# A graph layer beside a transformer on one core: the edge sort moved out of the input pass

## The chip, the cores and the metric

The kernel runs on one core of a Trainium2 chip. The metric is the time on the device in microseconds (us), as the median of several runs; lower is better. A profile of one execution belongs to it.

## The reference

For 6250 nodes of 256 features the kernel computes three things and adds them to the input. The first is an attention over 100,000 edges that go in by source node:

```python
feats = einsum('nd,hdo->hno', x, Ws) + bs            # 4 heads of 64
score = a_s[:, src] + a_d[:, dst] + aw_e * elem + ab
w = exp(-relu(score / 20))
pooled = segment_sum(w * feats[:, dst], src)         # by source node
out = pooled / segment_sum(w, src)
```

The second is a transformer of four layers on the same nodes, each with a linear attention (softmax of the queries over 32 features, of the keys over all nodes, one context matrix per head) and a feed-forward part of 1024 with GELU. The third is a slice attention on the sum of both. All is float32.

## The kernel before

All inputs are normalised first. Nodes are worked on in 50 tiles of 125 rows, in 13 groups: twelve of four tiles and one of two. There are six passes: the input pass (features of the graph layer, keys, queries and context of layer 0, and the table of features in DRAM), four layer passes (`attend`, `up`, `down`, and in the first three the keys, queries and context of the next layer), and the slice attention with its output. Layers are counted from 0; the first layer pass is layer 0, the last is layer 3.

The edge work is done beside the transformer, and that is what this case is about. It has three parts.

- The **sort** (`sort_step`, line 854) sorts edges by blocks of source tiles, on VectorE, in 59 steps. Steps 0 to 3 load and prepare; steps 4 to 28 count one pair of tiles each, with four passes over 125x800 (lines 884 to 888); step 32 (`COUNT_STEP`) makes prefix sums with two matmuls (line 1451) and a table of tiles that SP brings back from DRAM (line 515); steps 33 to 58 give each edge its place, 13 steps for each half of the edges, eight operations on 125x400 each (lines 926 and 927).
- The **scatter** (line 658): 800 indirect DMAs of GpSimd, 400 after each half is placed, write the records of the edges to DRAM in sorted order. Then `edges` loads them (line 525) and `rows` transposes the row numbers and stores them (line 529).
- The **edge blocks**: 220 blocks of 512 edges, in 224 pipelined items `("edge", k)`. Item k on TensorE makes the products of block k-4 (line 1486, eight matmul records) and the scores of block k-2 (line 1475); on VectorE it adds the sums (line 1154), makes the scores (958 to 963), the one-hot matrices (945, 951), and weighs the gathered features (941), which TensorE's item k+1 needs. GpSimd gathers features four blocks ahead (line 627). SP loads the rows of block k+2 in item k (line 445); line 951 waits for that.

All engines go through one list, `order`. It is made by hand: `stages` holds the transformer's stages with a cost in us that the author gave each (line 66 on), and `beside` holds the edge work with due times in the same clock. A beside item goes into the list before the first stage that begins at or after its due time. Each engine works the list in order. `mixed` is the planner's time at which the input pass ends (248.1), `added` that at which the last layer ends (2432.7). Before, sort steps are due from 20.0 on, every 16.0 in the input pass and every 7.5 behind it. The records are loaded 1.45 us for each of the 800 scatters behind the first half's last step; blocks are due evenly from there to `added`.

SP issues all other loads and stores in the order of the list too. Before each group of a layer it fetches the residual rows (line 412) and the stored queries (line 435) of the next group.

Of the kernel before, what the change touches and what calls it, by code (L numbers as in the profile page):

```python
# [10 lines left out]
def build_program(nc, x, src, dst, edge_weight, Ws, bs, aw, ab, Wq, Wk, Wv, Wo, bo, ln1_g, ln1_b, W1, b1, W2, b2,  # L11
# [46 lines left out]
    COUNT_STEP = 4 + NT // 2 + 3  # L58
# [31 lines left out]
    mixed = now()  # L90
# [26 lines left out]


    beside = []
    at = 20.0  # L120
    for k in range(SORT_STEPS):
        beside.append((at, ("sort", k)))
        at += 16.0 if at < mixed else 7.5
        if k == COUNT_STEP + HALF_STEPS:
            sorted_half = at
    edges_at = sorted_half + 1.45 * EC + 10.0
# [3 lines left out]
        beside.append((edges_at + 45.0 + k * (added - edges_at - 45.0) / (NB + 4), ("edge", k)))  # L130
    order, at = [], 0.0
    for item, us in stages:
        while beside and beside[0][0] <= at:
            order.append(beside.pop(0)[1])
        order.append(item)
        at += us
# [1485 lines left out]
```

How the kernel before makes its waits and increments, by code:

```python
            def load_x(p, s, source):  # L402
                slot, _ = x_loaded(p, s)
                if use(p, s) >= 3:
                    before = divmod(use(p, s) - 3, NGR)
                    if before[0] <= DEPTH:
                        e.wait_ge(*x_stored(*before))
                    else:
                        e.wait_ge(join_set, before[1] + 1)
                    if before[0] < DEPTH:
                        e.wait_ge(h1_set, nth(*before))
                e.dma_start(tiles_of(x_of(p, s), s), node_rows(source, s)).then_inc(slot, 16)
# [14 lines left out]
            def fetch(l, s):  # L427
                e.wait_ge(*x_stored(l, s))
                load_x(l + 1, s, x_d[l % 2])
                e.wait_ge(d_q, q_stored(l, s))
                if s:
                    e.wait_ge(v_done, v_end("attend", l, s - 1))
                elif l:
                    e.wait_ge(v_done, v_end("attend", l - 1, NGR - 1))
                e.dma_start(by_chunk(qT_in[:, :])[:, :, 0:cols_of(s)], q_rows(s)).then_inc(d_qin, 16)
# [4 lines left out]
            def load_rows_of(j):  # L440
                d_sem, _ = rows_in(j)
                if j >= 3:
                    e.wait_ge(ohT_set, j - 2)
                at = rows_d[TE * j:TE * (j + 1), :].rearrange("t p -> (t p)")
                e.dma_start(rows_ring[j % 3], at.partition_broadcast(R)).then_inc(d_sem, 16)
# [1 line left out]
            def fetch_sw(s):  # L447
# [1 line left out]
                if s < NSW:  # L449
                    e.wait_ge(d_sw, 16 * NGR)
                    e.wait_ge(v_done, v_end("slice_sums", NGR - 1))
                else:
```

## Time and profile before

| | us |
|---|---|
| median of 3 runs | 4057.73 |
| lowest and highest | 4050.81, 4059.79 |
| the profiled execution as a whole | 4050.51 |
| its span, first to last instruction | 4048.8 |
| TensorE busy | 3393.4 (84%) |
| VectorE busy | 2461.3 (61%) |
| GpSimd busy | 1950.4 (48%) |
| ScalarE busy | 1127.3 (28%) |

PE is TensorE, DVE VectorE, ACT ScalarE, POOL GpSimd, SP the engine that issues most DMAs. A line number such as L1486 is that of the kernel above. The busy time of pipelined matmuls overlaps a little. The granted clock (PEclk) is 1.00 for 2.4 GHz; single operations run at that or at 1.2 GHz.

### The profile page before, as it was taken

How to read it: one execution, taken by the hardware profiler on the slowest of the kernel's cores; microseconds unless marked ns; L12 is line 12 of the kernel's file. 1: busy time of each engine (PE TensorE's matmuls, PEld its weight loads, DVE VectorE, ACT ScalarE, POOL GpSimd, SP SyncE). 2: the span in 40 equal slices, each digit the busy share in tenths (PEclk: the TensorE clock that was granted, in tenths of full speed). 3: DMA queues.
4: the chain of work that ended last, by engine and by line, in shares of the span. 5: the costliest groups of instructions: out<-in, count | busy, mean ns of one | idle time of the engine just before them, and what ended most of it. 6: DMA issues, size and time to landing. Idle time of an engine off the chain costs nothing.

```text
span 4048.8 us, 44198 instructions
## 1 busy us (share of the span) xinstructions
PE 3393.4 (84%) x13941; PEld 2388.1 (59%) x13941; DVE 2461.3 (61%) x6828; ACT 1127.3 (28%) x1851; POOL 1950.4 (48%) x1745
## 2 busy tenths in 40 slices
PE   6887899999799999799888888777777677758989
PEld 4564666666566666566566566655455455545557
DVE  6886989644344444344677777665555455548951
ACT  2332232333233333223322222223223222312220
POOL 2120005777677777776356566555455455520000
PEclk8998999999899999899999999888888888979989
DMA  2222111221322222222344444444334434651224
GB/s 94 91 85 87 36 41 42 46 45 31 75 43 43 43 43 40 66 43 46 100 122 120 116 121 116 127 124 126 105 105 111 115 99 112 104 86 55 74 100 150
DMA packets 222382, 337.18 MB, mean 83 GB/s; under 512 B 49106, under 2 KB 175953, under 8 KB 221900
## 3 DMA queue, kind: packets, MB, share of 16 engines
q1 hardware_dynamic: 154316, 215.02, 17.0%
q0 software_dynamic: 67840, 119.33, 15.2%
q8 instruction: 119, 1.95, 0.2%
q14 instruction: 107, 0.88, 0.1%
HBM read 246.73 MB, written 86.62 MB: 82 GB/s over the span
## 4 chain that ended last, share of the span: by engine, by line
PE 57%; DVE 25%; DMA 5%; SPq 5%; issue 4%; ACT 3%; DVEq 1%; ACTq 0%
PE bank_v L1447 16%; PE bank_a L1432 12%; PE bank_e L1486 9%; DMA arena<-edge_rows 3%; PE bank_a L1353 3%; PE bank_v L1376 3%; PE bank_v L1339 3%; PE bank_v L1504 2%; PE bank_v L1594 2%; SPq L412 2%; DVE arena L941 2%; SPq L435 2%; PE bank_a L1280 2%; DVE st L813 1%; PE bank_v L1419 1%
## 5 line engine op out<-in xcount | busy, mean ns | idle before, releaser
L627 POOL DMA_INDIRECT arena<-gather_table,arena x880 | 919.6, 1045 | 769.9 <-PE bank_e L1486 541.5
L658 POOL DMA_INDIRECT edge_records<-acc x800 | 964.7, 1206 | 646.8 <-issue 646.8
L1486 PE MATMUL bank_e<-arena 128*125 128x260 f32 x1760 | 515.0, 442 | 284.1 <-DVE arena L941 284.0
L1432 PE MATMUL bank_a<-hT,W_sb 128*128 128x500 f32 (+1 forms) x1664 | 715.0, 581 | 38.3 <-ACT hT L677 24.7
L1447 PE MATMUL bank_v<-W_sb,gT 128*125 128x256 f32 x3200 | 735.8, 387 | 0.0
L1447 PEld LDWEIGHTS bank_v<-W_sb,gT 128*125 128x125 f32 x3200 | 602.6, 191 | 112.8 <-issue 23.4
L1486 PEld LDWEIGHTS bank_e<-arena 128*125 128x125 f32 x1760 | 355.6, 213 | 352.2 <-DVE arena L941 291.2
L1432 PEld LDWEIGHTS bank_a<-hT,W_sb 128*128 128x128 f32 x1664 | 319.2, 195 | 370.9 <-issue 314.0
L677 ACT ACTIVATE gT<-bank_a,cols 128x500 f32<-128x500 f32 (+1 forms) x416 | 274.4, 661 | 525.4 <-PE bank_a L1432 518.4
L677 ACT ACTIVATE hT<-bank_a,cols 128x500 f32<-128x500 f32 (+1 forms) x208 | 145.5, 748 | 750.7 <-PE bank_a L1280 750.4
L941 DVE TENSOR_TENSOR arena<-arena 128x1024 f32<-128x1024 f32 x220 | 267.7, 1217 | 0.0
L1154 DVE TENSOR_TENSOR acc<-acc,bank_e 125x260 f32 x440 | 184.6, 420 | 132.6 <-PE bank_e L1486 126.9
L1048 DVE TENSOR_REDUCE kst<-bank_a 128x1 f32<-128x500 f32 (+1 forms) x104 | 66.8, 656 | 293.6 <-PE bank_a L1353 293.1
L1115 DVE TENSOR_TENSOR xs<-bank_v,xs 125x512 f32<-125x512 f32 x100 | 69.0, 691 | 283.0 <-PE bank_v L1447 282.4
L762 ACT ACTIVATE arena<-esc 128x16 f32<-128x16 f32 x220 | 47.3, 215 | 656.1 <-DVE esc L963 655.1
L1419 PE MATMUL bank_v<-M_sb,qT_in 128*125 128x256 f32 x800 | 192.6, 395 | 30.7 <-issue 22.1
L1353 PE MATMUL bank_a<-hT,Wqkv 128*128 128x500 f32 (+1 forms) x416 | 184.6, 587 | 34.6 <-ACT hT L677 28.0
L1419 PEld LDWEIGHTS bank_v<-M_sb,qT_in 128*125 128x125 f32 x800 | 157.0, 197 | 63.5 <-issue 28.9
L1376 PE MATMUL bank_v<-h,ek 125*128 125x256 f32 x800 | 189.3, 391 | 0.0
L1142 DVE TENSOR_REDUCE esc<-bank_e 128x16 f32<-128x48 f32 x220 | 45.1, 205 | 232.3 <-PE bank_e L1486 231.1
L1280 PE MATMUL bank_a<-ident,h 125*128 125x125 f32 x900 | 124.4, 283 | 70.5 <-DVE h L837 58.8
L1339 PE MATMUL bank_v<-Wqkv,hT 128*125 128x256 f32 x800 | 181.2, 379 | 0.0
(261 smaller groups left out, 4388.3 us busy)
## 6 DMA issues: line engine op xcount, KB each, us to landing
residual<-xs SPq DMA_DIRECT2D x60, 500.0 KB
xs<-residual SPq DMA_DIRECT2D x60, 500.0 KB
arena<-edge_rows SPq DMA_DIRECT2D x220, 125.0 KB
queries<-qT_out SPq DMA_DIRECT2D x48, 500.0 KB, 3.6
qT_in<-queries SPq DMA_DIRECT2D x48, 500.0 KB, 14.0
arena<-gather_table,arena POOLq DMA_INDIRECT x880, 3.5
edge_records<-acc POOLq DMA_INDIRECT x800
slice_weights<-arena SPq DMA_DIRECT2D x12, 1000.0 KB, 5.0
```

The costliest lines, as they stand in the source:

```text
L627: e.indirect_dma_start(g_of(j)[:, i, :], None, table_d, bass.IndirectOffsetOnAxis(ap=rec[:, TE * j + i, 0:1].bitcast(I32), axis=0))\
L658: e.indirect_dma_start(rec_d, bass.IndirectOffsetOnAxis(ap=pos_i[:, f:f + 1], axis=0), r3[:, f, :], None).then_inc(d_rec, 16)
L677: e.activation(to, of, func, **k).then_inc(a_done, 1)
L941: e.tensor_tensor(gf, gf, bc(g[:, :, HG * DG:ROW].unsqueeze(3), [P, TE, HG, DG]), ALU.mult)\
L1280: o = e.transpose(b[:, i * R:(i + 1) * R], X[:, i, c * P:(c + 1) * P], ident[0:R, 0:R])
L1339: o = e.matmul(b[0:R, i % 2 * D:(i % 2 + 1) * D], hv[:, k, i * R:(i + 1) * R], W[:, k, 0:D], start=k == 0, stop=k == KC - 1)
L1353: o = e.matmul(b[:, 0:n], W[:, k, D + c * P:D + (c + 1) * P], hv[:, k, 0:n], start=k == 0, stop=k == KC - 1)
L1376: o = e.matmul(b[:, c * D:(c + 1) * D], ek[:, a:a + P], h1[:, i * D:(i + 1) * D], start=i == 0, stop=i == tiles(s) - 1)
L1419: o = e.matmul(to, qv[:, k, i * R:(i + 1) * R], M_sb[:, k * D:(k + 1) * D], start=k == 0, stop=k == KC - 1)
L1432: o = e.matmul(b[:, 0:n], W[:, k, f * P:(f + 1) * P], hv[:, k, 0:n], start=k == 0, stop=k == KC - 1)
L1447: o = e.matmul(b[0:R, i % 2 * D:(i % 2 + 1) * D], gv[:, f, i * R:(i + 1) * R], W2_sb[:, f * D:(f + 1) * D], start=False, stop=f == FB - 1 ...
L1486: o = e.matmul(ps_sum[h], oh_ring[j % 4][:, i * R:(i + 1) * R], g_of(j)[:, i, :], start=i == TH * h, stop=i == TH * (h + 1) - 1)
```

## The change

The sort's first step becomes due 20 us before the input pass ends, and all steps follow at 7.5. Three of them still fall into the pass (0, 1 and 2); the others lie in layer 0, into its tenth group. Since the record load and the blocks are placed by the sort's end, they move back by 80.6 planner us, and the 224 items lie at 2.877 instead of 3.237. The second edit keeps step 32, which fills a PSUM bank of its own, from standing between the two halves of a `down` pair, which share one.

```diff
     beside = []
-    at = 20.0
+    at = mixed - 20.0
     for k in range(SORT_STEPS):
         beside.append((at, ("sort", k)))
-        at += 16.0 if at < mixed else 7.5
+        at += 7.5
         if k == COUNT_STEP + HALF_STEPS:
             sorted_half = at
...
     for item, us in stages:
-        while beside and beside[0][0] <= at:
+
+        whole = item[0] != "down" or item[3] % 2 == 0
+        while beside and beside[0][0] <= at and (whole or beside[0][1] != ("sort", COUNT_STEP)):
             order.append(beside.pop(0)[1])
```

## Rows read from the trace of the kernel before

**Rows 1.** The page: busy time by engine, chain that ended last

```profile
PE 3393.4 (84%) x13941; PEld 2388.1 (59%) x13941; DVE 2461.3 (61%) x6828; ACT 1127.3 (28%) x1851; POOL 1950.4 (48%) x1745
...
PE 57%; DVE 25%; DMA 5%; SPq 5%; issue 4%; ACT 3%; DVEq 1%; ACTq 0%
```

**Rows 2.** Stretches of the input pass: length, busy by engine, clock, DMA share, GB/s

```profile
91.50:332.30 240.80, 207.57 (x918) 147.46 (x917) 208.86 (x570) 83.78 (x180) 41.38 (x35) 0.94 0.28 94
170.10:191.40 21.30, 19.68 (x94) 14.24 (x93) 19.23 (x55) 8.14 (x17) 4.83 (x4) 1.00 0.27 92
```

**Rows 3.** Timeline: start, length, operation, in brackets the idle time before

```profile
107.98 1.09 PE L1280 MATMUL bank_a<-ident,h 125*128 125x125 f32 x4 [5.21 <-ACT qT_out L677]
...
102.84 0.58 DVE L862 CAST acc<-acc 125x800 f32<-125x800 int32 x1 [5.57 <-DMA acc<-in_edge_weight]
```

**Rows 4.** Stretches of layer 0: seven groups, single groups, one without steps

```profile
405.60:762.30 356.70, 329.60 (x1308) 229.18 (x1307) 317.69 (x769) 107.56 (x166) 95.51 (x75) 0.99 0.17 41
457.90:512.10 54.20, 48.19 (x188) 33.34 (x187) 51.09 (x103) 15.67 (x24) 0.00 (x0) 0.97 0.13 38
659.70:713.70 54.00, 48.08 (x186) 33.37 (x186) 49.92 (x131) 15.56 (x24) 41.94 (x33) 0.97 0.22 40
859.30:907.90 48.60, 46.24 (x188) 32.25 (x187) 21.74 (x68) 15.56 (x24) 37.10 (x32) 1.00 0.24 45
```

**Rows 5.** Timeline at the end of the input pass, VectorE and TensorE

```profile
354.41 0.98 DVE L884 SCALAR_TENSOR_TENSOR acc<-acc 125x800 f32<-125x800 f32 x1
...
359.39 0.17 DVE L1094 RECIPROCAL kst<-kst 128x2 f32<-128x2 f32 x1
...
360.27 1.12 PE L1386 MATMUL bank_a<-ident,kh 128*128 128x128 f32 x4 [6.69 <-DVE kh L1096]
...
372.28 1.19 PE L1419 MATMUL bank_v<-M_sb,qT_in 128*125 128x256 f32 x2 [4.76 <-issue]
```

**Rows 6.** Stretches with edge blocks; the last two are L1486 alone (eight per block)

```profile
1952.70:2620.50 667.80, 552.94 (x2456) 406.68 (x2455) 490.04 (x1410) 186.07 (x319) 385.22 (x370) 0.93 0.42 114
2131.80:2223.90 92.10, 77.88 (x355) 57.23 (x354) 70.31 (x207) 25.95 (x44) 58.33 (x57) 0.96 0.46 123
2700.80:3573.30 872.50, 644.24 (x2643) 456.27 (x2642) 486.83 (x1400) 239.92 (x329) 456.89 (x437) 0.86 0.43 108
...
1952.70:2620.50 667.80, 208.19 (x736) 0.93 0.42 114
2700.80:3573.30 872.50, 262.77 (x873) 0.86 0.43 108
```

**Rows 7.** Timeline of TensorE in the last layer, around blocks

```profile
3256.13 3.83 PE L1486 MATMUL bank_e<-arena 128*125 128x260 f32 x8 [2.85 <-DVE arena L941]
...
3263.34 3.83 PE L1486 MATMUL bank_e<-arena 128*125 128x260 f32 x8 [3.29 <-DVE arena L941]
...
3287.75 2.02 PE L1486 MATMUL bank_e<-arena 128*125 128x260 f32 x8
3289.60 3.52 PE L1432 MATMUL bank_a<-hT,W_sb 128*128 128x500 f32 x8
...
3293.14 2.02 PE L1486 MATMUL bank_e<-arena 128*125 128x260 f32 x8
...
3421.14 2.00 PE L1486 MATMUL bank_e<-arena 128*125 128x260 f32 x8
...
3426.52 2.02 PE L1486 MATMUL bank_e<-arena 128*125 128x260 f32 x8 [3.22 <-DVE arena L941]
```

**Rows 8.** Scatter by line; SP's timeline; a wait of VectorE: total, times, longest

```profile
L658 POOL DMA_INDIRECT edge_records<-acc x800: 1182/1187/2103, 642.1 to 1913.6; - x160
...
1926.38 0.42 SPq L525 DMA_DIRECT2D arena<-edge_records  x1
3290.10 7.30 SPq L412 DMA_DIRECT2D xs<-residual  x1
...
DVE arena L951 <- DMA arena<-edge_rows: 135.6, 12, 22.1
```

## The prediction

> **What bounds the kernel now.** I read the page first: the busy shares and the chain [rows 1]. TensorE is busy 84% of the span of 4048.8 us and is 57% of the chain, VectorE is 25% of it. So a saved VectorE microsecond counts only where TensorE waited for it, and each stretch must be asked alone. The run that was profiled took 4050.5 us as a whole, 1.7 us around its span; the three timed runs have the median 4057.7, so it stands 7.2 us below it. My sum is a difference; I add it to both.
>
> The stretch view, cut at the start of each group of four node tiles, gives the prices of stages. In the pass over the input ten groups from 91.5 to 332.3 us take 240.8 us; one that TensorE fills at full clock takes 21.3 [rows 2]. In the first layer an undisturbed group takes 48.6 us with VectorE busy 21.7; one with dense sort steps takes 54.2 with VectorE busy 51.1 [rows 4]. In the edge stretch, the products of 92 blocks of layer 2 (736 records of eight to a block) and of 109 of the last layer fall into 667.8 and 872.5 us [rows 6].
>
> **The change, part one: the input pass.** Where the counting steps lie is worked out from the planner's own costs (a plain sum of its numbers). Before, steps 1 to 14 lie in the pass; after, only 0, 1 and 2, in its last two groups. The stall that they make: step 1 waits 5.57 us for the edge load, runs five operations, and TensorE stands 5.21 us, its next operations at the lower of its two clocks [rows 3]. Ten groups at 21.3 are 213.0 us, so the pass can give back 240.8 - 213.0 = **27.8 us** [rows 2]. I take all of it: groups with one step in a harmless place ran at 21.3 already. Of the DMAs that move with step 0 (three edge loads, the blank records), SP issues them some 20 us ahead of the last group, where no group waits for them; the weight loads of the first layer come behind. POOL's two blanking memsets now come after its last normalisation, where it has nothing else. Both at nothing; if that cover were gone, the price is the 5 us stall of [rows 3].
>
> **Part two: the boundary.** Before, step 14 (4.98 us, first operation at 354.41, next work at 359.39) lies right before the key sums are finished, and TensorE waits for that until 360.27 [rows 5]. After, step 2 is there, which has ten full-width operations; at 0.58 us [rows 3] to 0.98 us [rows 5] each I estimate 6 to 10 us for it, 1 to 5 more than now. Step 1 is before the last keys, where step 13 was a stage earlier, worth 0 to 2. Behind it TensorE waits 4.76 us for the query load anyway [rows 5], which hides most: **+2 us**, bounds 0 and +7.
>
> **Part three: the first layer.** It now holds 56 steps, not 44. A counting step takes 4.98 us of VectorE [rows 5], the planner puts 6.1 into a group (46.0 of its us at one per 7.5; undisturbed it takes 48.6), so a dense group asks VectorE for 21.7 + 6.1 x 4.98 = 52.1 us, against 48.6 of the group: VectorE becomes the bound there, by 3.5 us, and 54.2 is what such a group took [rows 4]. Before, two groups are dense and seven with steps take 356.7 us, 16.8 over seven undisturbed. After, three groups are full of counting steps and a fourth half (18 us over), and three of the groups behind have a step right before the queries; the one group of that kind before took 54.0, 5.4 over [rows 4]. Two counted in full, one at 4.5, and 1.5 for the last: 18 + 15.3 + 1.5 = 35, less 16.8 gives 18. Most steps fall in kinder places than the worst of before, so I take **+15 us**, bounds +6 and +22. The wait that moves with the count step (SP for the tile table) only moves; queued behind it is one fetch of a group, a stage ahead of its use, at nothing.
>
> **Part four: the scatter.** Its 800 issues run from 642.1 to 1913.6 and SP reads the records at 1926.4, behind its own fetch [rows 8]. The first half's last step moves 82.4 planner us (486.1 to 568.5), the record load 80.6 (1664.0 to 1744.6). At 48.6 / 46.0 these are 87 and 85 us: the slack of about 12 us shrinks by 2, and by what layer 0 is late, which moves both. At nothing; if the slack goes, each further us is paid.
>
> **Part five: the edge blocks, which decide.** They start 80.6 planner us later and end where they did, so their pitch falls from 3.237 to 2.877. TensorE's work of one block is small: from one block's start to the next with two up-projections between is 5.39 us, 3.52 of it those two, so 1.87 is the block [rows 7]. But two blocks with nothing between are also 5.38 apart, with TensorE idle 3.22 [rows 7]: block k+1 needs the weighted features that VectorE makes after block k's products. So 5.4 us is a floor that the pitch must not undercut, and the new pitch (2.877 x 48.6/46.0 = 3.04 us of other work, with the block 4.9) is under it, the old (3.42, 5.3) about at it. By the list of the order: pairs with nothing between go from 20 to 33, blocks with one up-projection between from 5 to 20, with only a transpose stage from 1 to 3. Each leaves TensorE idle for the missing work: 3.5, 1.8 and 2.4 us. That is 81 us before and 159 after, **+77**.
>
> Two credits. First, every group of the last layer has one wait for the rows of the edges, twelve in all, 135.6 us [rows 8], since SP's fetches block the row loads behind them (issuing one takes 7.30 us [rows 8]). It is a wait for DMA from a fixed point, so short intervals inside it cost nothing: 13 of the up-projection kind and three of the transpose kind, 30 us; but in half of the groups one up-projection less is done when the wait begins, 11 us back. **-20.** Second, 1.75 groups of layer 2 are no longer mixed with blocks. In 667.8 us, bare layer work is about 350 (five and a half groups at 48.6 and two shorter ones at the end, estimated at 80 together), blocks 92 x 1.87 = 172, short intervals some 33; the other 113 over seven groups are 16 a group, the stalls after a normalisation. **-28.** Sum for the edges: 77 - 20 - 28 = **+29**; a second tally, group by group (a group of 14 blocks takes 92.1, one of 16 then 104 to 109; the eleven last-layer groups of 9.9 blocks take 79.3 on the mean [rows 6], one of 11 then 81 to 83), gives +25. I take **+27**, bounds: 0, if a block costs the same wherever it lies, and +50, if the pairs run at the lower clock. For that last the rows have both: the pair at 3256.13 and 3263.34 is 7.21 us apart, its products taking 3.83 us for the same work that takes 2.02 at 3426.52 [rows 7]. That is 1.2 against 2.4 GHz after TensorE had stood idle for some us.
>
> The Trainium skill (TensorE: Matmul & The Clock Gate, section A second HAM failure mode: psum-queue depth-cycling) says that frequent small idle times between matmul groups can make the clock swing between its levels and cost throughput between bursts. It speaks against the change, since that makes many such gaps; by the rows it holds for some pairs and not for others. If it held for all 15 new short intervals outside the DMA wait (31 new ones less the 16 inside), at 1.8 us each (7.21 - 5.39), the edges would be +54 instead of +27.
>
> **Sum:** -28 + 2 + 15 + 0 + 27 = **+16 us**: 4066.5 for the profiled execution, 4074 for the median.
>
> **The rivals.** (B) Low clock at the new short intervals: 15 intervals at 1.8 us more by the pair at 7.21 us, 27 us, so 4101 for the median. For it: the granted clock is 0.86 over the last layer already [rows 6]. Against: the pair at 3426.52 runs at full clock. (C) The other side: a block has one price wherever it stands. Its mechanism is that the chain from VectorE to TensorE is covered by work that only changes place, so that each stall made at the tighter pitch is one saved in the groups that are no longer mixed. The place is the stretch from 1953 us on; with edges at 0 the sum is -28 + 2 + 15 = -11 us, 4047, and 4038 with the first layer at its lower bound; it decides once the edges cost less than 11 us. For it: [rows 6] show (667.8 - 350) / 92 = 3.5 us over the bare work per block in layer 2, which is near what a block plus its share of stalls must cost anywhere. Against it: the same 5.4 us in the pair and in the covered interval. (D) The scatter ends after SP asks for the records: decided by 12 us of slack; one that ends 20 us late costs 8 beyond my sum, 4082. (E) Intervals with one up-projection are no case for the floor, because their neighbours lend cover. Then their 27 us go, and of the first credit the 12 that belong to them: edges +12, sum +1, 4059. That the change doesn't do what it says is small: the order says that three steps stay in the pass.
>
> **Chances.** A 0.45, B 0.10, C 0.20, D 0.05, E 0.20. The range that holds 8 in 10 goes from between C's 4047 and its 4038, at 4042, to just above B, 4104; A alone is 4064 to 4090. About 0.2%, 8 us, is what a measurement can tell from none. Faster: C most of it, 0.22. Same: E and A's lower end, 0.25. Slower: 0.53.
>
> **What would show it.** Right: input groups from the third on at 21 to 22 us, three or four first-layer groups at 52 to 55, VectorE over 90% there; scatter from about 710 to 1980; layer-2 groups of 16 blocks at 104 to 110 and last-layer groups of 11 at 80 to 83; the layer-2 edge stretch about 25 shorter and the last layer about 50 longer. Wrong: input groups still at 25 (then the stalls weren't the sort's); last-layer groups at 77 (then a block costs nothing more); a row wait in layer 2, or twelve that are longer than 11.3 us each. The largest risk is part five, a count of intervals priced by a few rows.

## The result, and the profile after

The change makes the kernel slower. Its median is 4103.4 us (4099.7 to 4111.8, four runs) against 4058.1 for the kernel before, a ratio of 1.0118 with a 95% interval of 1.0097 to 1.0139. The forecast was 4074 in a range of 4042 to 4104, so the direction was right and the size, 16 us against 45, too small. The profiled execution has a span of 4099.1 us where before has 4048.8: +50.3.

First the page of after: busy times of the engines and the chain that ended last, to be laid beside [rows 1].

```profile
span 4099.1 us, 44194 instructions
...
PE 3428.8 (84%) x13941; PEld 2414.7 (59%) x13941; DVE 2464.0 (60%) x6828; ACT 1124.0 (27%) x1847; POOL 1949.9 (48%) x1745
...
PE 60%; DVE 23%; DMA 4%; SPq 4%; issue 3%; ACT 3%; DVEq 1%; ACTq 0%
```

VectorE has the same work to 3 us. TensorE has the same instructions and is busy 35 us longer for them, which points to a lower clock somewhere.

Now stretches: the same ten groups of the input pass as in [rows 2], one of them, three dense groups of layer 0 as in [rows 4], then the edge stretches of [rows 6]: layer 2 from its first mixed group, one group of 16 blocks, groups 0 to 10 of the last layer. The columns are those of before.

```profile
91.50:292.10 200.60, 195.36 (x918) 142.02 (x918) 152.54 (x505) 84.29 (x180) 44.82 (x37) 1.00 0.31 104
171.30:191.40 20.10, 19.58 (x94) 14.29 (x93) 15.97 (x55) 8.47 (x18) 4.85 (x4) 1.00 0.32 108
419.50:577.90 158.40, 144.27 (x566) 99.76 (x565) 149.12 (x314) 46.83 (x72) 0.00 (x0) 0.98 0.13 39
...
2026.80:2680.60 653.80, 502.58 (x2127) 367.54 (x2126) 444.43 (x1273) 165.10 (x279) 361.93 (x348) 0.88 0.41 112
2135.00:2247.60 112.60, 89.08 (x379) 64.97 (x378) 77.69 (x227) 29.07 (x48) 66.50 (x64) 0.89 0.42 113
2680.60:3612.60 932.00, 692.57 (x2812) 492.19 (x2811) 536.73 (x1540) 247.77 (x347) 514.38 (x493) 0.86 0.45 111
```

The input pass takes 200.6 us for ten groups where it took 240.8 [rows 2]. In layer 0 three dense groups take 158.4, which is 52.8 each, with VectorE busy 94% of it. In the last layer eleven groups take 932.0 where they took 872.5 [rows 6].

Cut at the points at which a layer's key sums are finished, the difference of the two executions is this. Each row is the length of that stretch after, less that before.

| stretch | before | after | difference |
|---|---|---|---|
| start to the end of the input pass | 360.3 | 326.1 | -34.2 |
| layer 0 | 655.2 | 664.1 | +8.9 |
| layer 1 | 643.3 | 642.9 | -0.4 |
| layer 2 | 966.1 | 964.7 | -1.4 |
| last layer up to its twelfth group | 948.4 | 1014.8 | +66.4 |
| rest | 475.5 | 486.5 | +11.0 |

So the front gives 26 us, and the part with the edge blocks takes 76. The next line is the group of the blocks' products in after, all 220 blocks, with the start of the first and of the last record. Before, it is the same form with 1995.6 to 3622.5.

```profile
L1488 PE MATMUL bank_e<-arena x1760: 382/383/798, 2057.0 to 3670.5; 128*125 128x260 f32 x196
its engine sat idle before it (us, times) until:
  DVE arena L943: 308.4, 89
```

I call the time from the first block's products to the last's the **edge stretch**. It was 1626.9 us and is 1613.5. This gives the result in three terms: the blocks start 61.4 us later (25.7 us were gained in front, so the delay itself is 87.1, for 80.6 of the planner's us), the stretch is 13.4 shorter, and what lies behind it is 2.3 longer. 61.4 - 13.4 + 2.3 = 50.3. The delay was meant to be repaid by the tighter pitch. It wasn't.

### The profile page after: what moved, and what is told of

Same layout as the page of the kernel before. It is cut to its first block, busy times and chain, and to the rows that moved or that the text cites. A ratio compares the mean times of both kernels' runs of the same rounds, so it can differ in the third digit from the quotient of the medians.

```text
span 4099.1 us, 44194 instructions
## 1 busy us (share of the span) xinstructions
PE 3428.8 (84%) x13941; PEld 2414.7 (59%) x13941; DVE 2464.0 (60%) x6828; ACT 1124.0 (27%) x1847; POOL 1949.9 (48%) x1745
## 4 chain that ended last, share of the span: by engine, by line
PE 60%; DVE 23%; DMA 4%; SPq 4%; issue 3%; ACT 3%; DVEq 1%; ACTq 0%
PE bank_v L1449 15%; PE bank_a L1434 12%; PE bank_e L1488 9%; PE bank_a L1355 4%; PE bank_v L1378 4%; DMA arena<-edge_rows 3%; PE bank_v L1341 3%; PE bank_v L1506 2%; PE bank_a L1282 2%; DVE arena L943 2%; PE bank_v L1596 2%; SPq L437 2%; DVE st L815 2%; SPq L414 2%; ACT hT L679 1%
## 5 line engine op out<-in xcount | busy, mean ns | idle before, releaser
L1488 PE MATMUL bank_e<-arena 128*125 128x260 f32 x1760 | 544.2, 462 | 308.4 <-DVE arena L943 308.4
L1449 PE MATMUL bank_v<-W_sb,gT 128*125 128x256 f32 x3200 | 746.4, 391 | 1.1 <-issue 1.1
L1488 PEld LDWEIGHTS bank_e<-arena 128*125 128x125 f32 x1760 | 374.4, 224 | 384.7 <-DVE arena L943 316.8
L1421 PEld LDWEIGHTS bank_v<-M_sb,qT_in 128*125 128x125 f32 x800 | 156.3, 196 | 61.4 <-issue 22.5
L1341 PEld LDWEIGHTS bank_v<-Wqkv,hT 128*125 128x125 f32 x800 | 151.2, 189 | 40.0 <-issue 19.4
```

Source lines behind the costliest of these rows:

```text
L1341: o = e.matmul(b[0:R, i % 2 * D:(i % 2 + 1) * D], hv[:, k, i * R:(i + 1) * R], W[:, k, 0:D], start=k == 0, stop=k == KC - 1)
L1421: o = e.matmul(to, qv[:, k, i * R:(i + 1) * R], M_sb[:, k * D:(k + 1) * D], start=k == 0, stop=k == KC - 1)
L1449: o = e.matmul(b[0:R, i % 2 * D:(i % 2 + 1) * D], gv[:, f, i * R:(i + 1) * R], W2_sb[:, f * D:(f + 1) * D], start=False, stop=f == FB - 1 ...
L1488: o = e.matmul(ps_sum[h], oh_ring[j % 4][:, i * R:(i + 1) * R], g_of(j)[:, i, :], start=i == TH * h, stop=i == TH * (h + 1) - 1)
```

## The experiments

Each ratio is against the kernel before on the same chip in the same session. Microseconds of two sessions are not compared as they stand, since before itself moved between them. The medians of before there were 4106.7 us (sort_late to before_split), 4063.5 (before_o to before_split_xo), 4091.8 (after_fill7 to before_dense), 4059.2 (before_weigh to the best one), 4053.3 (the last two). Differences under 0.3% between sessions are not read.

### Which half costs: the sort's place or the blocks'

**sort_late** has the new sort and the blocks where they were.

```diff
-    edges_at = sorted_half + 1.45 * EC + 10.0
+    edges_at = 1662.5
```

> The sort moved as in the change, the edge blocks left where they were before (same start, same pitch, same list of pairs). So that the records are there in time, the last 160 of the 800 scatters are left out; the edges' part of the output lacks their records. Theory 1 (the front of the kernel gains, the blocks lose): input pass 34 us shorter, layer 0 9 us longer, edge stretch as before, so 25 us faster than before (22 to 28). Theory 2 (the later sort itself costs, through GpSimd or DMA beside it, and the blocks' place is innocent): 25 to 50 us slower than before.

Measured: 4084.4 us, ratio 0.9941 (0.992 to 0.9961), 24 us less than before.

**edges_late** has the old sort and `edges_at = 1743.125`, the value that after has.

> The sort left as before, the record load and the blocks put at the planner times of the change (1743.1 and pitch 2.877). Theory 1: the front is as before, the edge stretch as after, so 76 us slower than before (70 to 82) and 25 slower than the change. Theory 2: as before, within 10 us.

Measured: 4175.4 us, ratio 1.0164 (1.0126 to 1.0201), +67 us by the ratio, a little under the 70 to 82 expected. The two halves add up to 1.0105, near the 1.0118 of the whole. The front's gain is real, and moving the blocks is what costs. It does so with the old sort too, so it isn't the later sort or the later scatter.

### Are adjacent blocks the cost

**after_split** and **before_split** put no block right behind another and none ahead of `h1` or `total`; it comes one stage later.

```diff
-        while beside and beside[0][0] <= at:
+        while beside and beside[0][0] <= at and not (item[0] in ("h1", "total") or order and order[-1][0] == "edge"
+                                                     and beside[0][1][0] == "edge" and beside[0][1][1] > 3):
             order.append(beside.pop(0)[1])
```

> The change with one more rule in the list: a block is not put right behind another, but one stage later. Pairs go from 33 to 1, blocks with one up-projection between from 20 to 61, with a transpose stage from 3 to 18; pitch and number are the same. If every short interval costs just the missing work up to 5.4 us (3.5, 1.8, 2.4), the sum stays (159 to 157 us): within 8 us of the change. If a pair costs about 5.8, as the trace of after has it (184 us over 32 pairs, against 106 over 20), each pair broken up saves 2 to 2.3: 60 to 75 us faster than the change, about 4035.

> The kernel before with the same rule: pairs from 20 to 0, one up-projection between from 5 to 27, a transpose stage from 1 to 16. Missing work alone: 81 to 87 us, so 6 us slower than before. Pairs dear by themselves: 20 x 2.3 less 6, 40 us faster than before.

Measured: after_split 4067.8 us, ratio 0.989 (0.9856 to 0.9924); before_split 4018.6, ratio 0.9781 (0.9738 to 0.9825). Both gain about 90 us. But the change costs as much between these two, 1.1%, as between the originals, although one pair is left in one and none in the other. Pairs aren't what the change costs. The size surprised me, too: 20 pairs can't hold 88 us by the floor of 5.4 us. In layer 2 next to nothing was gained; in the last layer eleven groups took 71.9 us on the mean, and 80.4 in sort_late on the same chip. The wait of VectorE for the row numbers of the edges tells why. Total us, times, longest; in [rows 8] it is 135.6, 12, 22.1.

```profile
DVE arena L952 <- DMA arena<-edge_rows: 47.8, 15, 13.7
```

The rule also puts a block between `total` and the fetches at `up` 0, and so a row load between two bursts of SP.

**before_o** does only that half (nothing ahead of `h1` and `total`, all 20 pairs stay), and **before_xo** keeps the blocks and takes one of the two bursts away: the load for `total` goes to the sixth `up`.

```diff
                     store_x(DEPTH, s, x_d[DEPTH % 2])
-                    if s + 1 < NGR:
-                        load_xo(s + 1)
...
                     if f == 0 and s + 1 < NGR:
                         fetch(l, s + 1)
+                    if f == 5 and l == LAST and s >= 1:
+                        load_xo(s)
```

> The kernel before, and nothing changed but the place of a block that is due before a `total` or an `h1`: it comes behind it, so between `total` and the fetches at `up` 0, one per last-layer group. All 20 pairs of blocks stay. Theory P (the gain of before_split is the place of that block: SP gets a row load out between its two bursts, and the wait for rows shrinks): 60 to 85 us off the kernel before, ratio 0.979 to 0.985, last-layer groups of 10 blocks at 70 to 73. Theory Q (the gain was that no two blocks are adjacent): at most 10 us off, ratio 0.997 to 1.0, groups still at 77 to 80.

> The kernel before; only SP's load of the input rows for `total` (512 KB per group) moves from the `total` stage to the sixth `up` of the last layer, away from the fetches at `up` 0. All blocks stay where they are. Theory P in its wider form (each last-layer group pays once for the burst of loads in front of a row load): the wait for rows falls from 135.6 us to 30 to 60, 60 to 90 us off, ratio 0.978 to 0.985. If the fetches at `up` 0 alone already make the wait: at most 25 us off, ratio above 0.994.

> before_split (no block right behind another, none before `h1` or `total`) with the load of the input rows moved to the sixth `up` as well. If both edits remove the same wait for rows: ratio as before_split, 0.975 to 0.981, since only 47.8 us of that wait are left in it. If the load was still in front of a row load there: 20 to 40 us more off, ratio 0.968 to 0.974.

Measured: before_o 4039.3, ratio 0.9942 (0.992 to 0.9964): 24 us, so the place alone is a quarter of it and my expectation missed. before_xo 4004.7, ratio 0.9851 (0.9829 to 0.9873): 61 us, with the row wait at

```profile
DVE arena L951 <- DMA arena<-edge_rows: 68.3, 11, 16.1
```

which is 67 us less than in [rows 8]. before_split_xo, both edits: 3922.9, ratio 0.9662 (0.964 to 0.9684). They nearly add up (0.9781 times 0.9851 is 0.9635): the two together take 48 us more off than before_split does, where I had expected none or 20 to 40. 14.3 us of row wait are left.

**after_split_xo** is the same on after.

> after_split with the load of the input rows moved to the sixth `up`. It says what the change costs when both the pairs and the wait for rows are gone. If the tighter pitch costs by pairs and row waits alone, it is as fast as before_split_xo or up to 15 us faster (the front's 25 us stay): ratio 0.961 to 0.967. If every block added to a group costs more than one it takes from an unmixed group, wherever it is put: ratio 0.973 to 0.980, that is, the change still costs some 40 us.

Measured: 4014.1, ratio 0.9815 (0.9788 to 0.9842), 1.6% above before_split_xo (0.9815 / 0.9662). With row waits of 13.0 and 14.3 us and at most one pair, the change costs at least as much as it did. So its cost is neither in the pairs nor in the row waits. (The two intervals together leave about 0.4% on each side, so 1.6% isn't clearly more than 1.2%.)

### Is the low clock the cost

In after, the products of 66 blocks take over 2.6 us, as against 44 before; they take up to 3.83 where others take 2.0. 30 of the 66 are in the 32 adjacent blocks (counted block by block in the timeline). Here is one of them, with the VectorE work between: start, length, operation, idle time before it.

```profile
3454.21 2.00 PE L1488 MATMUL bank_e<-arena 128*125 128x260 f32 x8
3455.37 0.21 DVE L1144 TENSOR_REDUCE esc<-bank_e 128x16 f32<-128x48 f32 x1 [1.78 <-PE bank_e L1488]
...
3456.42 0.43 DVE L1156 TENSOR_TENSOR acc<-acc,bank_e 125x260 f32 x1 [0.51 <-PE bank_e L1488]
...
3456.76 0.17 DVE L960 TENSOR_TENSOR esc<-arena,awe 128x16 f32<-128x16 f32 x1
...
3457.47 0.67 DVE L947 TENSOR_TENSOR arena<-iota_row,arena 128x500 f32<-128x500 f32 x1
...
3458.05 0.35 DVE L953 TENSOR_SCALAR arena<-arena,iota_part 125x512 bf16<-125x512 bf16 x1
3458.32 1.22 DVE L943 TENSOR_TENSOR arena<-arena 128x1024 f32<-128x1024 f32 x1
...
3459.59 3.83 PE L1488 MATMUL bank_e<-arena 128*125 128x260 f32 x8 [3.22 <-DVE arena L943]
```

TensorE does nothing for 3.22 us, and the next products run at the lower level. It isn't so each time: in before, 15 of the 20 pairs had products over 2.6 us, and the others, with the same idle time, kept 2.0.

**after_fill** gives it something to do there, with nobody waiting for the result. **after_fill7** and **before_fill7** have 7 instead of 14 matmuls.

```diff
                         j = k - 4
+                        for i in range(14 if k in close else 0):
+                            e.matmul(bank_e[0][0:R, 320:512], oh_ring[j % 4][:, 0:R], oh_ring[j % 4][:, 0:192],
+                                     start=True, stop=True)
                         e.wait_ge(p_set, j + 1)
```

`close` is the list of blocks that stand right behind another.

> The kernel after; in the 32 blocks that stand right behind another, TensorE runs 14 extra matmuls of 125x192 (about 0.19 us each at full clock, 2.6 us in all) into unused columns of bank_e while it waits for the weighed features. Nothing waits for their result. Rival B (the short idle time drops the clock, and this is what the pairs cost): blocks at the low clock fall from 66 to 30 to 40, a pair takes 5.4 instead of 7.2 us, 40 to 55 us less than after, ratio to before 0.998 to 1.002. Theory A (a floor of 5.4 us and nothing more; the low clock is a symptom that costs nothing): as after, ratio 1.010 to 1.014; if the extra work itself delays the block, up to 10 us more.

> As after_fill with half the extra matmuls: 7 of 125x192 in each of the 32 adjacent blocks. In after_fill the 14 took 4.79 us at full clock, longer than the wait of 3.3 us they were to fill, so a pair took 6.6 us. 7 should take 2.4 us. If the clock is what the pairs cost (rival B): pairs at 5.4 to 5.6 us, low-clock blocks at 30 to 40 as there, 45 to 55 us less than after, ratio to before 0.998 to 1.001. If 2.4 us of work are too little to hold the clock: blocks at the low clock back at 60 or more and the time of after, ratio 1.010 to 1.014.

> The kernel before with the same 7 extra matmuls in its 19 adjacent blocks, 15 of which ran at the low clock. Rival B: 15 times 1.8 us, 20 to 27 us less than before, ratio 0.993 to 0.995. With after_fill7 this gives the cost of the change when the pairs keep their clock: 18 to 25 us of the 48. Theory A: no difference, ratio 0.999 to 1.001.

Measured: after_fill 4097.1, ratio 1.0081 (1.0062 to 1.0101). That is 15 us less than after by the ratios, and fits neither expectation. No adjacent block ran at the low clock any more, but the 14 matmuls took 4.79 us, more than the wait they filled:

```profile
3452.07 4.79 PE L1486 MATMUL bank_e<-arena 128*125 128x192 f32 x28
```

The count tells why I had them too cheap: a float32 matmul leaves two records here (the four of a block leave eight), so the 14 are 28 records of 0.17 us each. In after_fill7 the ratio is 1.0021 (1.0007 to 1.0034), some 40 us less than after; in before_fill7 it is 0.9933 (0.9911 to 0.9955), 27 us less than before. TensorE's timeline of such a pair in after_fill7:

```profile
3460.70 2.00 PE L1493 MATMUL bank_e<-arena 128*125 128x260 f32 x8
3462.53 0.32 PE L1479 MATMUL bank_e<-as,arena 125*128 x4
3462.71 2.52 PE L1486 MATMUL bank_e<-arena 128*125 128x192 f32 x14
3466.08 2.02 PE L1493 MATMUL bank_e<-arena 128*125 128x260 f32 x8 [0.85 <-DVE arena L945]
```

The pair is 5.4 us apart, not 7.2, though TensorE did 2.5 us more, and one of the 32 pairs is left with products over 2.6 us, where 30 were. So the clock fell because of the idle time, and it costs what its rows say. But before pays it as well: with the pairs warm in both, the change still costs 1.0021 / 0.9933, 0.9% or 36 us of the 48. The low clock at pairs is 40 us of after and only about 12 us of the change. The Trainium skill (TensorE: Matmul & The Clock Gate, section A second HAM failure mode: psum-queue depth-cycling) describes a clock that swings between its two levels when TensorE is idle for short times between groups of matmuls, and throughput lost by it. These runs agree: 30 of 32 pairs low without the extra work, one with it, and 40 us between the two kernels.

### The pitch, the start, or the chain

By now three causes had each failed to hold the change's cost. Two kernels move start and pitch apart.

**before_dense**: first block as before, the pitch of after.

```diff
-        beside.append((edges_at + 45.0 + k * (added - edges_at - 45.0) / (NB + 4), ("edge", k)))
+        beside.append((edges_at + 45.0 + k * (added - 80.6 - edges_at - 45.0) / (NB + 4), ("edge", k)))
```

> The kernel before with its sort, its scatter and its first block where they are, but the pitch of after (2.877): the blocks end 80.6 planner us earlier and the last three and a half groups of the last layer have none. Pairs are 35, as against 20. It tells the pitch from the later place. If the pitch is what costs (more blocks in each group, pairs with nothing between): ratio 1.010 to 1.018, with last-layer groups of 11 blocks at 82 to 90 and the unmixed ones at the end at 32 to 38 us giving back less than the dense ones take. If a block costs the same wherever it stands (rival C): ratio 0.997 to 1.003.

**edges_early**: `edges_at = 1581.9`, first block earlier by what edges_late has it later, and the pitch wider.

> The kernel before with record load and blocks 80.6 planner us earlier than before (1581.9), the mirror of edges_late; so that the records are there, the second half's scatter stops at 640 of 800, so 160 issues of GpSimd are left out. Pairs 7 instead of 20, pitch 3.6 instead of 3.24. Theory F (start plus a chain of about constant length): first products 85 us earlier, the stretch 15 to 30 us longer, 50 to 70 us off, ratio 0.983 to 0.988. Theory W (the reckoning of the prediction: 13 fewer pairs at 3.5 us, 1.75 more mixed groups at 16): 45 less 28, 17 us off, ratio 0.996.

Measured: before_dense 4180.2, ratio 1.0218 (1.0193 to 1.0242), worse than after itself. edges_early 3969.7, ratio 0.977 (0.9746 to 0.9793), better than I expected. The products' line in before_dense:

```profile
L1486 PE MATMUL bank_e<-arena x1760: 382/383/799, 1995.1 to 3639.4; 128*125 128x260 f32 x196
```

and in edges_early:

```profile
L1486 PE MATMUL bank_e<-arena x1760: 382/383/799, 1917.9 to 3541.2; 128*125 128x260 f32 x196
```

| kernel | first products | last products | edge stretch | planner's pitch | median of before in that session |
|---|---|---|---|---|---|
| edges_early | 1917.9 | 3541.2 | 1623.3 | 3.60 | 4059.2 |
| before | 1995.6 | 3622.5 | 1626.9 | 3.24 | 4058.1 |
| after | 2057.0 | 3670.5 | 1613.5 | 2.88 | 4058.1 |
| before_dense | 1995.1 | 3639.4 | 1644.3 | 2.88 | 4091.8 |
| sort_late | 1982.1 | 3658.7 | 1676.6 | 3.24 | 4106.7 |
| edges_late | 2091.4 | 3739.1 | 1647.7 | 2.88 | 4106.7 |

The planned length of the stretch goes from 806 to 645 planner us. The first three rows, whose sessions had the same before, stay between 1613 and 1627 us. The last three were slower sessions. There edges_late is 29 us shorter than sort_late, which has the blocks where before has them, for some 85 us of the transformer's work taken out. In before_dense the last three and a half groups of the last layer were put behind the stretch. What lies behind it takes 523.7 us where it took 426.3 in before, and the kernel as a whole is 2.2% slower, 89 us, so the stretch gave little of that back. Most of the time of work that leaves the stretch comes on top.

That points to the blocks' own chain. In the fence of the pair above it can be read: products (2.0 us), VectorE's reduction and two additions, the scores of another block (0.17 each), two one-hot matrices (0.67 and 0.35), then the weighing (1.22), and only then the next products. One turn is 5.38 us with nothing else in it. The intervals between the blocks' products don't shrink with the pitch: their mean is 7.42 us in before and 7.36 in after, the median 5.95 and 6.82, and 89 and 79 of the 219 take 5.5 us or less.

The chain doesn't hold the whole stretch, though. Two up-projections and a block also fill 5.39 us of TensorE by themselves [rows 7], so an interval of 5.4 us with these between doesn't tell which of the two set it. TensorE is seen waiting for the weighed features 89 times in after (308.4 us, in the fence with all 220 blocks above) and 76 times in before:

```profile
PE bank_e L1486 <- DVE arena L941: 284.0, 76, 24.1
```

Some of this is the wait for the rows of the edges handed on, since line 951, which waits for them, stands ahead of the weighing. The stretch as a whole, before and after, in the columns of [rows 2]:

```profile
1995.60:3622.50 1626.90, 1265.06 (x5420) 918.10 (x5417) 1030.24 (x2985) 451.50 (x688) 904.04 (x864) 0.89 0.44 113
2057.00:3670.50 1613.50, 1223.61 (x5085) 884.71 (x5083) 994.55 (x2874) 423.82 (x646) 901.14 (x864) 0.87 0.45 112
```

Some 84 us of planned transformer work left the stretch (219 intervals, 0.36 planner us each, at 48.6 / 46.0). TensorE's busy time in it fell by only 41.5, as the clock went from 0.89 to 0.87, and its idle time grew by 28.

The scores and the one-hot matrices are not needed by the next products, and still stand in front of the weighing. **before_weigh** and **after_weigh** put them behind it. The edit does two things: it shortens the chain, and it takes the wait of line 951 for the rows out of the way of the next products.

```diff
+                    if 3 <= k <= NB + 2:
+                        weigh(k - 3)
                     if 2 <= k <= NB + 1:
                         scores(k - 2)
                     if k < NB:
                         one_hot(k)
                         one_hot_T(k)
-                    if 3 <= k <= NB + 2:
-                        weigh(k - 3)
```

> The kernel before; VectorE weighs the features of block k-3 (1.22 us) right behind its two additions, ahead of the scores and the one-hot matrices (1.8 us), where it came last in the item. Same work, same order of stages. Theory F (from its first block the kernel takes as long as the blocks' own chain, products, additions, weighing, products, takes for 220 of them; 1627 us from the first products to the last before, 1614 after): each step of the chain is up to 1.4 us shorter, so the stretch takes 1430 to 1550 and the time falls by 80 to 200 us, ratio 0.951 to 0.980. Theory W (only intervals with too little TensorE work in them pay): the 20 adjacent pairs gain 1.4 us each, ratio 0.991 to 0.995.

> The kernel after with the same edit of VectorE's item. Theory F: the later start costs 61 us less 14 because the chain has no room at the tighter pitch; with the shorter chain it has room, so against before_weigh the change costs at most 25 us or gains, and against the kernel before the ratio is 0.951 to 0.985. Theory W: 33 pairs gain 1.4 us each, 46 us less than after, ratio to before about 1.0.

Measured: before_weigh 3980.2, ratio 0.9801 (0.9783 to 0.9819); after_weigh 3988.0, ratio 0.9821 (0.9802 to 0.984). Moving two lines brings 2.0% and 2.9%, and between these two the change costs 0.2%, where it cost 1.2%. That 0.2% flatters the change: before_weigh has a wait of TensorE for the stored queries, about 8 us in most groups of the last layer, that is not there in before and is 1.6 us in after_weigh.

```profile
PE bank_v L1419 <- DMA qT_in<-queries: 91.6, 9, 28.1
```

So this pair of kernels can't price the change. The last two kernels below, which have no such wait, can. The products in before_weigh and after_weigh:

```profile
L1486 PE MATMUL bank_e<-arena x1760: 382/383/799, 1991.6 to 3553.0; 128*125 128x260 f32 x196
```

```profile
L1488 PE MATMUL bank_e<-arena x1760: 382/383/798, 2055.3 to 3558.8; 128*125 128x260 f32 x196
```

The stretch is now 1561.4 and 1503.5, 57.9 shorter for a start 63.7 us later, but most of that difference may be the wait for the queries. A pair in before_weigh, TensorE and the weighing:

```profile
3351.88 2.00 PE L1486 MATMUL bank_e<-arena 128*125 128x260 f32 x8
...
3354.43 1.22 DVE L941 TENSOR_TENSOR arena<-arena 128x1024 f32<-128x1024 f32 x1
...
3355.70 2.02 PE L1486 MATMUL bank_e<-arena 128*125 128x260 f32 x8 [1.67 <-DVE arena L941]
```

It is 3.82 us apart, TensorE idle 1.67, and the clock stays up. It doesn't in all of them: 10 of the 20 pairs are still low, where 15 were. The gain of before_weigh, 79 us by the medians, is at the low edge of what I expected. The shortest intervals with two up-projections went from 5.4 to 5.3 only, since there TensorE's own work (3.52 and 1.87) is the limit, the row wait grew from 135.6 to 165.4 us, and the wait for the queries is new.

### The best version

> before_split_xo with VectorE's edit. Its stretch took 1494 us from the first products to the last. Theory F: another 60 to 150 us off, ratio to before 0.930 to 0.952, unless the attention's normalisation (intervals of 11 to 12 us, once or twice a group) or TensorE's own work takes over first. Theory W: no pairs are left, so nothing: 0.966.

> after_split_xo with VectorE's edit (weighing right behind the additions). Theory F: with the blocks' chain as it was the change cost 1.5% here (after_split_xo 0.9815, before_split_xo 0.9662); with the shorter chain it costs at most half of that, ratio to before 0.942 to 0.950 beside 0.942 of before_split_xo_weigh. If the change costs by something else that the chain doesn't hold: 0.955 or more.

> before_xo with VectorE's edit, blocks where they are, 20 adjacent pairs kept. An adjacent pair now takes 3.8 us and not 5.4, so pairs should no longer matter: ratio 0.942 to 0.950 if so. If breaking them still brings what it brought without the edit (before_xo 0.9851, before_split_xo 0.9662): 0.958 to 0.965.

Measured: **before_split_xo_weigh 3821.0 us, ratio 0.9421 (0.9402 to 0.9439)**, faster than both kernels by 238 us and more. after_split_xo_weigh 3839.8, ratio 0.947 (0.944 to 0.95): the change costs 0.5% here (0.947 / 0.9421, good to about 0.4%), where it cost 1.6% with the old order of VectorE's item. It doesn't gain there either. These two have next to no row wait (32.5 and 28.1 us), no wait for the queries and at most one pair. The products, and the stretch as a whole, in before_split_xo_weigh and after_split_xo_weigh:

```profile
L1487 PE MATMUL bank_e<-arena x1760: 382/383/799, 1994.2 to 3391.7; 128*125 128x260 f32 x196
1994.20:3391.70 1397.50, 1213.00 (x5421) 888.05 (x5417) 1034.45 (x2985) 464.28 (x698) 889.47 (x864) 0.94 0.52 131
```

```profile
L1490 PE MATMUL bank_e<-arena x1760: 382/383/798, 2061.1 to 3410.4; 128*125 128x260 f32 x196
2061.10:3410.40 1349.30, 1136.98 (x5080) 830.24 (x5080) 992.38 (x2857) 461.04 (x674) 899.33 (x864) 0.94 0.55 134
```

The start is 66.9 us later and the stretch 48.2 shorter, and TensorE's busy time in it falls by 76.0, at the same clock. With the old order, in before_split_xo and after_split_xo, the start was 64.5 later and the stretch 22.9 longer (1494.1 and 1517.0), in a session that by its before was 28 us slower. Those two have next to no row wait either, so it is the shorter chain that does it: with it the tighter pitch repays most of the delay.

before_xo_weigh is at 3897.5 us, ratio 0.9603 (0.9578 to 0.9628): breaking the pairs brings 1.9% with the short chain (0.9421 / 0.9603), as much as with the long one. That was the outcome I thought less likely, since a pair costs 3.8 us here. Part of it is the row wait, 85.4 us in before_xo_weigh and 32.5 in the best one, while the stretch is 81 us shorter (1478.5 and 1397.5). For the other 28 us there is one candidate in the traces, not tested: before_xo_weigh has 28.8 us of TensorE waiting for the stored queries, the best one none.

The page of the best version, to be laid beside [rows 1]:

```profile
span 3817.8 us, 44206 instructions
...
PE 3341.8 (88%) x13941; PEld 2358.4 (62%) x13941; DVE 2466.7 (65%) x6828; ACT 1140.3 (30%) x1861; POOL 1937.3 (51%) x1745
```

## Why the prediction came out as it did

**Part one and two, the front: right, and too careful.** Forecast -28 and +2; the pass with its boundary took 34.2 us less. The price of a group that TensorE fills at full clock was read as 21.3, from a group with a sort step in it. Without steps it is 20.1, so ten groups gave 40.2 and not 27.8. From the end of those groups to the finished key sums it takes 34.0 us where it took 28.0, so the boundary costs 6 and not 2, still within the bounds of 0 and 7.

**Part three, layer 0: right in kind, 6 us too dear.** Forecast +15, measured +8.9. Seven groups with steps took 51.9 to 54.1 us, as forecast, 29.7 us over undisturbed ones where the sum had 35; and the layer's first group was reached 3.7 us sooner.

**Part four, the scatter: right in its price, wrong in its slack.** It ended 57 us later, but SP came to the records only 48 us later (1926.4 and 1974.0), so the slack of 12 us was used up, where the forecast took 2 off it. SP waited for the last records:

```profile
SPq L527 <- DMA edge_records<-acc: 2.7, 1, 2.7
```

The first products came 83 us behind that, so no time is seen to hang on it. Rival D decided nothing, by luck rather than by the forecast slack.

**Part five, the edges: the sign right, the size not.** Forecast +27, measured +76. The step that failed is the price of the short intervals, +77 in the sum. To see this I took off each of the 219 intervals the planned cost of what stands in it (at 48.6 / 46.0) and 1.87 us for the block. What is left over is 464 us in before and 534 in after. By kind of interval:

| interval | before | after | measured difference | forecast |
|---|---|---|---|---|
| short: nothing, one up-projection or one transpose between | 124.7 (26 of them) | 241.3 (55) | +117 | +57 (77 less the first credit, 20) |
| all others | 339.6 | 293.0 | -47 | -28 (the second credit) |

Together they are +70 of the 76; the row waits lie in both kinds. The other 6 us are the delay, 87.1 where 83.5 of work left, and the 2.3 behind the stretch.

- **The step: each short interval was charged the work missing up to 5.4 us, and no more.** That is 3.5 us for a pair and 1.8 for one up-projection. A pair left over 5.0 us on the mean in both kernels, and an interval with one up-projection 4.3 and 3.6. A pair took 6.9 us on the mean, not 5.4, as its products mostly ran at the low clock and some pairs took over 10 us.
- **Behind it stands a wrong picture: that intervals can be priced one by one.** With all pairs but one broken up the change still costs 1.1%, and the tighter pitch alone, with no later start, costs 2.2% (before_dense). What takes most of the cost away is to shorten VectorE's part of the item: 1.6% becomes 0.5%. So the stretch is held in large part by the blocks' chain from TensorE to VectorE and back, and work that leaves it mostly doesn't shorten it but comes on top.
- I had both rows side by side [rows 7] and took the 5.4 us of the covered interval for a sign of the floor. It is TensorE's own work, 3.52 and 1.87, that happens to fill as much.
- The first credit, 20 us, was for short intervals hidden inside the row wait. That wait fell by about as much, from 135.6 to 114.4 us, but no run isolates what was hidden in it. The second, 28 us for 1.75 groups no longer mixed, was not too large: the other intervals gave 47. It was the short ones that took it back. Layer 2 was to be 25 us shorter and is 1.4 shorter: its other intervals gave 21 back, and its short ones took 45 more, where their share of the forecast is 22. The two groups with the products of 16 blocks took 112.6 and 112.7, where the forecast had 104 to 110.
- The low clock (rival B) was given 27 us and a chance of 0.10. It is there in 30 of 32 pairs, and worth 12 us of the change by the fill runs, because most of the pairs of before had it too. TensorE's busy time is 35 us longer in all, so there is low clock outside the pairs as well. With the pairs filled in both kernels most of that is gone too (3475.6 against 3437.1 us busy, of which 12 pairs more of 2.52 us are 30), and 36 us of the change's cost stay.

Looking back, a plainer reckoning comes out near: 87 us of delay, less 26 of the front, less a little, is 50 to 60. It was made with the result known.

Rival C, a block that costs the same wherever it stands, was given 0.20 and had the mechanism upside down. The mean interval does stay nearly the same (7.42 and 7.36 us). What changes its price is the transformer's work, cheap inside the stretch and paid in full outside it. Rival E, +12 for the edges, is excluded by the 76. The upper bound of the edges, +50, left the measured +76 out. The whole came within the range, less than 1 us under its upper end, only because the front gave 26 us where 11 were forecast. That was luck.

Of the forecast signs, the input groups at 20 to 21 us, the dense groups of layer 0 and the scatter were right. Last-layer groups of 11 blocks were to take 80 to 83; the eleven groups took 71 to 96, 84.7 on the mean.

## What to carry to other kernels

Where pipelined items are spread between other work, read the time from one item's end to the next over all of them before pricing a new pitch. If their mean stays where it is when less work stands between them, the items' own chain is a large part of the bound: a tighter plan repays little, and most of the work moved out of the stretch is paid. Then shorten the chain first. One value with and without work between is no proof by itself; see whether the work alone would fill it. Here an operation that the next item doesn't need stood ahead of one that it does. And a small transfer that someone waits for should not stand behind two large bursts on one queue: here moving one of the two brought 61 us. After each such edit look for the wait that takes over, as the queries' load did in before_weigh.

## What the runs showed of the hardware

- An idle time of 2.8 to 4.2 us on TensorE, 3.2 in most, was followed by products above 2.6 us, up to 3.83 (1.2 GHz), in 30 of the 32 adjacent blocks of after and 15 of the 20 of before. With the shorter chain the idle time is 1.3 to 1.7 us in most, and 13 of 32 and 10 of 20 were still low (after_weigh, before_weigh), most of them behind the shortest, about 1.3 us. So the idle time just before isn't all that counts. With 2.52 us of unneeded matmuls in the gap one of 32 and one of 20 were, and adding this work made both kernels faster, by 40 and 27 us.
- A float32 matmul leaves two records. With 192 columns a record took 0.17 us (4.79 for the 28 of 14 matmuls), with 260 columns 0.25 (2.00 for eight).
- A load of 512 KB, moved by about 10 us of the plan on SP's queue, took 67 us of row waits away, nearly all in the groups of the last layer.
- The same kernel, before, had medians from 4053 to 4107 us in these sessions, 1.3% apart, more than the whole effect of the change. One chip gave 4106.7 in one session and 4063.5 in the next, so it isn't the chip alone. Kernels of two sessions can't be compared to half a per cent.
